# A hybrid attention and mixture-of-experts block on one core: the shared expert's first two token chunks are placed between the two halves of the routing logits

## The chip, the cores and the metric

The kernel runs on one core of one Trainium2 chip. The metric is the device time of one execution in microseconds (us), the median of three runs. One further execution was taken by the hardware profiler; all durations below come from that one.

## The reference, cut to what matters

Eleven layers run one after the other on 2 x 1024 tokens of width 128: three attentions of a first block with two Fourier feed-forwards, then a location attention, a mixture of experts, a masked linear layer, a ReLU attention, a feed-forward with ReLU, and a second mixture of experts. The change touches the two mixture-of-experts layers only. Each computes, in float32, with `xt` the layer-normed tokens:

```python
scores = jax.nn.sigmoid(xt @ gate_w.T)                 # 16 experts
_, idx = lax.top_k(scores + gate_b, 4)
w = take_along_axis(scores, idx); w = w / sum(w) * 2.5
comb = zeros((T, 16)).at[arange(T)[:, None], idx].add(w)
def expert_body(y, (w13_e, w2_e, c_e)):
    h = silu_and_mul(xt @ w13_e.T)                     # 128 -> 2 x 64
    return y + c_e[:, None] * (h @ w2_e.T)
y = scan over the 16 experts
y = y + silu_and_mul(xt @ w13_s.T) @ w2_s.T            # the shared expert, no routing
```

## The kernel before, in words

Activations lie transposed, width on the 128 partitions and tokens along the free axis, in four chunks of 512 tokens. It is written by hand, one instruction stream for each engine, with named semaphores; each engine runs its stream in program order. The streams are below `@block.tensor` (TensorE, `pe`), `@block.scalar` (ScalarE, `act`), `@block.vector` (VectorE, `dve`), `@block.gpsimd` (GpSimd, `pool`) and `@block.sync` (SyncE, `sp`, which issues the DMAs). Every matmul but a transpose goes through the helper `mm` at line 1639, so the profile knows them all by that line and they are told apart by operands and shape. A float32 matmul of the program is two MATMULs in the profile.

A mixture-of-experts layer (`moe_layer`, called "layer 1" for i = 0 and "layer 2" for i = 1) follows a layer norm. The norm leaves its centred chunk c in PSUM bank c and its variance in bank 4 + c; VectorE multiplies bank c by the factor into `z` (line 1158) and counts `n_z`, so `n_z` at 4n + c + 1 says that chunk c of `z` is there and that bank c may be overwritten.

TensorE then runs, in this order:
- the routing logits, lines 2030 to 2036: for each of 16 tiles of 128 tokens a matmul with `z` as the stationary side and `gate_w` (16 columns) moving, all into bank 4; `n_z` is waited for at the first tile of each chunk, and the last matmul counts `m_log`;
- `ahead(a)` for a = 0 to 9 (lines 2041 to 2052). For a = 0 and 1 this is the shared expert's gate and up projections of token chunks 2a and 2a + 1, 64 output rows each, into the halves of bank a (gate) and bank 2 + a (up); for a = 2 to 9 it is the gate and up projection of expert pair a - 2 for chunk 0. From a = 2 on it waits for `e_a`, which ScalarE counts when it has emptied the banks of a - 2. Each ends with a count on `e_gu`;
- after `ahead(5)`, `ahead(6)` and `ahead(7)` the `route_rows` (line 2069): transposes (line 2072) of the combine weights of chunks 0 and 1, of chunk 2, and of chunk 3. They wait for `m_d`, which VectorE counts through the 12 steps of the routing;
- the loop over `PAIRS`: gate and up projections of chunks 1 to 3 (`gate_up`), the shared expert's down projection (`shared_down`, once per chunk, which waits for `m_cs`) and the experts' down projections (`down`).

ScalarE (line 1043) waits for `m_log`, takes the exponential of the 16 x 16 logits (line 1045), then for each a applies SiLU to the gate bank (line 1057) and copies the up bank (line 1058, counts `e_a`). A table load stands before the first SiLU. Behind a = 6, 7, 8 it copies the transposed combine weights (line 1050, counts `m_cs`). GpSimd (line 753) multiplies the two results into the hidden rows, one product for each a. VectorE (lines 1499 to 1530) turns the exponentials into combine weights: add, reciprocal, bias, top-8 for each of 16 tiles (1509), match-and-replace for each (1517), compare (1520), products, sum, reciprocal, and a last scaling (1528). It then starts the loop over `PAIRS` with line 1553, hidden rows times the combine weights that SyncE has stored to DRAM and loaded back spread over 64 partitions (lines 550 to 575).

Of the kernel before, what the change touches and what calls it, by code (L numbers as in the profile page):

```python
# [31 lines left out]
T = B * S  # L32
# [3 lines left out]
P = 128  # L36
# [15 lines left out]
NE, INTER, TOPK = 16, 64, 4  # L52
# [50 lines left out]
def build(nc, xt, wp, vp, cp, bp, rope_q, rope_k, bias_q, bias_k, out):  # L103
    ctx = ExitStack()
    with ctx:
# [3 lines left out]
        def sem(name):  # L109
            return ctx.enter_context(nc.semaphore(name))  # L110
# [4 lines left out]
        h, z = hz[:, 0:T], hz[:, T:2 * T]  # L115
# [61 lines left out]
        def bank(i):  # L177
            return ps[:, i, :]
# [4 lines left out]
        def w_(name, rows=P):  # L183
            a, b = WAT[name]
            return wsb[0:rows, a:b]
# [11 lines left out]
        def c_(name, rows=P):  # L197
            a, b = CAT[name]
            return csb[0:rows, a:b]
# [8 lines left out]
        def ch(t, c):  # L208
            return t[:, c * CH:(c + 1) * CH]
# [14 lines left out]
        s_late = sem("late_weights_and_constants_loaded")  # L224
# [11 lines left out]
        n_z = sem("norm_done")  # L236
# [33 lines left out]
        m_log = sem("route_logits")  # L270
# [21 lines left out]
            mm=sem("proj_in_psum"),  # L292
            t=sem("rope_products"),
# [129 lines left out]
        def full(i, c, j):  # L423

            return (i * (NC - 1) + c - 1) * NPAIR + j
# [21 lines left out]
        AHEAD = 2 + NPAIR  # L447
# [44 lines left out]
        def weights_of(v):  # L492

            return work[:, (4 + v % 3) * S:(5 + v % 3) * S]
# [1142 lines left out]
        def _(pe):  # L1637
            def mm(o, l, r, start=True, stop=True):
                return nc.tensor.matmul(o, l, r, start=start, stop=stop, skip_group_check=True)  # L1639
# [387 lines left out]
                    mm(bank(4 + c), lhs, ch(z, c)).then_inc(s_lin, 1)  # L2027

            def moe_layer(i, n):
                for t in range(T // P):  # L2030
                    if i + t == 0:
                        pe.wait_ge(s_late, 32)
                    if t % 4 == 0:
                        pe.wait_ge(n_z, 4 * n + t // 4 + 1)
                    ins = mm(bank(4)[:, t * NE:(t + 1) * NE], z[:, t * P:(t + 1) * P], w_("gate_w"))
                ins.then_inc(m_log, 1)

                wg, wu = [w_(name)[:, NPAIR * P:NPAIR * P + INTER] for name in ("w_gate", "w_up")]
                wd = w_("w_down")[:, NPAIR * P:NPAIR * P + P]

                def ahead(a):

                    if a >= 2:
                        pe.wait_ge(e_a, AHEAD * i + a - 1)
                    if a < 2:
                        for o, w in ((bank(a), wg), (bank(2 + a), wu)):
                            for half in range(2):
                                ins = mm(o[HB * half:HB * (half + 1)], w, ch(z, 2 * a + half))
                    else:
                        mm(bank(a % 2), w_("w_gate")[:, (a - 2) * P:(a - 1) * P], ch(z, 0))  # L2050
                        ins = mm(bank(2 + a % 2), w_("w_up")[:, (a - 2) * P:(a - 1) * P], ch(z, 0))
                    ins.then_inc(e_gu, 1)

                def shared_down(c):

                    rows = slice(INTER * (c % 2), INTER * (c % 2 + 1))
                    pe.wait_ge(e_m, AHEAD * i + c // 2 + 1)
                    mm(bank(4 + c), wd[rows], moe[rows, 5, c // 2], True, False)

                def gate_up(c, j):  # L2060
                    f = full(i, c, j)
                    if c == 1 and j < 2:
                        pe.wait_ge(e_a, AHEAD * (i + 1))
                    else:
                        pe.wait_ge(m_su, f - 1)
                    mm(bank(f % 2), w_("w_gate")[:, j * P:(j + 1) * P], ch(z, c))
                    mm(bank(2 + f % 2), w_("w_up")[:, j * P:(j + 1) * P], ch(z, c)).then_inc(m_gu, 1)

                def route_rows(c):
                    pe.wait_ge(m_d, ROUTE_STEPS * (i + 1))  # L2070
                    for tt in range(4):
                        ins = nc.tensor.transpose(bank(4 + c)[0:NE, tt * P:(tt + 1) * P],  # L2072
                                                  rt[:, (4 * c + tt) * NE:(4 * c + tt + 1) * NE], c_("ident"))
                    ins.then_inc(m_t, 1)

                def down(n):
                    c, j = PAIRS[n]
                    k = ITEMS * i + n
                    pe.wait_ge(m_h, k + 1)
                    return mm(bank(4 + c), w_("w_down")[:, j * P:(j + 1) * P], moe[:, 2, k % 2], False, j == NPAIR - 1)  # L2080

                if i == 0:
                    pe.wait_ge(s_ws, 16)
                for a in range(AHEAD):
                    ahead(a)
                    for c in ROUTE_AT.get(a, ()):
                        route_rows(c)
                for n, (c, j) in enumerate(PAIRS):
                    if c or n == 0:
                        for ahead_of in [p for p in PAIRS[n + 1:] if p[0]][0:1]:  # L2090
                            gate_up(*ahead_of)
                    if j == 0:
                        pe.wait_ge(m_cs, NC * i + c + 1)
                        shared_down(c)
                    down(n).then_inc(m_y if j < NPAIR - 1 else s_lin, 1)
# [25 lines left out]
            for c in range(NC):  # L2121
                pe.wait_ge(n_z, 4 * 6 + c + 1)
                mm(bank(c), w_("loc_w"), ch(z, c)).then_inc(l_xt, 1)
                for tt in range(4):
                    t = 4 * c + tt
                    ins = nc.tensor.transpose(bank(4 + c)[:, tt * P:(tt + 1) * P], z[:, t * P:(t + 1) * P],
                                              c_("ident"))
# [3 lines left out]
            for v in range(B * KT + 2):  # L2131
                if v < B * KT:
# [3 lines left out]
                    for half in range(2):  # L2136
                        ins = mm(bank(2 * (v % 2) + half), z[:, v * P:(v + 1) * P], ch(xtr, CB * b + half))
                    ins.then_inc(l_s, 1)
                if v >= 2:
# [3 lines left out]
                    for half in range(2):  # L2143
                        ins = mm(bank(4 + CB * b + half), zr[:, u, :],
                                 weights_of(u)[:, half * CH:(half + 1) * CH], u % KT == 0, u % KT == KT - 1)
# [3 lines left out]
            for c in range(NC):  # L2149
                ins = mm(bank(0)[32 * c:32 * c + 32], c_("ones")[:, 0:32], ch(dacc, c))  # L2150
            ins.then_inc(l_den, 1)
            pe.wait_ge(d_v, 1)
            for c in range(NC):
                mm(bank(c), c_("first_row")[32 * c:32 * c + 32], inverse[32 * c:32 * c + 32]).then_inc(d_r, 1)
            norm(7)
            moe_layer(0, 7)
            norm(8)
            pe.wait_ge(s_fb, 7)
# [6 lines left out]
            for c in range(NC):  # L2165
# [7 lines left out]
                for j in range(FF // P):  # L2173
                    pe.wait_ge(f_r, 4 * c + j + 1)
                    ins = mm(bank(4 + c), w_("ff2")[:, j * P:(j + 1) * P], ffh[:, c % 2, j], j == 0, j == 3)
                ins.then_inc(s_lin, 1)
            norm(12)
            moe_layer(1, 12)


# [190 lines left out]
```

## Time and profile before

| | |
|---|---|
| median of 3 runs | 1020.58 us (1020.56 to 1021.92) |
| profiled execution, its own time | 1023.21 us |
| its span in the trace | 1021.1 us |
| mean granted TensorE clock | 0.948 of full |
| TensorE busy | 948.7 us, 93% |
| VectorE / ScalarE / GpSimd busy | 535.3 (52%) / 540.0 (53%) / 147.7 (14%) us |
| the first mixture-of-experts layer's logits start | at 570.3 us of the span |
| the second one's | at 916.5 us |

The span is the time between the first and the last instruction in the trace; the execution's own time has 2.1 us around it. PEclk is the share of the full TensorE clock of 2.4 GHz that was granted in a stretch, so 0.50 is 1.2 GHz. "Busy" counts an engine as busy while an instruction is on it, however little of it the instruction uses. A timeline row merges neighbouring instructions of one kind; where other engines' instructions come between, a merged row can span them, and its duration includes the last one's run to its end.

### The profile page before, as it was taken

How to read it: one execution, taken by the hardware profiler on the slowest of the kernel's cores; microseconds unless marked ns; L12 is line 12 of the kernel's file. 1: busy time of each engine (PE TensorE's matmuls, PEld its weight loads, DVE VectorE, ACT ScalarE, POOL GpSimd, SP SyncE). 2: the span in 40 equal slices, each digit the busy share in tenths (PEclk: the TensorE clock that was granted, in tenths of full speed). 3: DMA queues.
4: the chain of work that ended last, by engine and by line, in shares of the span. 5: the costliest groups of instructions: out<-in, count | busy, mean ns of one | idle time of the engine just before them, and what ended most of it. 6: DMA issues, size and time to landing. Idle time of an engine off the chain costs nothing.

```text
span 1021.1 us, 22819 instructions
## 1 busy us (share of the span) xinstructions
PE 948.7 (93%) x9990; PEld 436.0 (43%) x9990; DVE 535.3 (52%) x870; ACT 540.0 (53%) x767; POOL 147.7 (14%) x164
## 2 busy tenths in 40 slices
PE   7698978999999988988998999989999999999998
PEld 4476733433333335754443444434333333444443
DVE  4576545523324375665565525555666666423554
ACT  6044535889999856443765531256455454445121
POOL 3001120501001003120010120000223322004000
PEclk9899989899999997589998799999999999899999
DMA  7644050100000000000000057100000000001651
GB/s 205 215 128 125 7 218 0 42 2 2 2 2 2 2 1 1 3 3 2 0 1 0 1 135 138 62 1 1 2 2 2 2 2 2 0 1 43 160 123 52
DMA packets 16763, 43.16 MB, mean 42 GB/s; under 512 B 4844, under 2 KB 5292, under 8 KB 15244
## 3 DMA queue, kind: packets, MB, share of 16 engines
q1 hardware_dynamic: 15692, 39.51, 14.5%
q10 hardware_dynamic: 972, 2.20, 0.7%
q8 instruction: 79, 1.29, 0.5%
q14 instruction: 20, 0.16, 0.1%
HBM read 36.91 MB, written 4.55 MB: 41 GB/s over the span
## 4 chain that ended last, share of the span: by engine, by line
PE 82%; ACT 8%; DVE 6%; issue 2%; DMA 1%; POOL 1%; ACTq 0%; SPq 0%; DVEq 0%; POOLq 0%
PE ps L1639 82%; ACT nrr L816 1%; ACT nrr L818 1%; ACT nsq L809 1%; DVE mxq L1258 1%; ACT work L897 1%; POOL work L677 1%; ACT nrr L826 0%; ACT nrr L823 0%; DMA stf<-scr_k 0%; DVE aux L1451 0%; DVE work L1307 0%; DMA x<-in_x 0%; PE ps L2072 0%; DVE work L1363 0%
## 5 line engine op out<-in xcount | busy, mean ns | idle before, releaser
L1639 PE MATMUL ps<-rq,stf 32*64 32x512 f32 (+4 forms) x4096 | 208.4, 465 | 3.3 <-ACT hz L1001 1.6
L1639 PE MATMUL ps<-work,vbuf 64*32 64x128 f32 (+6 forms) x2992 | 195.5, 421 | 2.4 <-DVE nsq L1357 2.2
L1639 PE MATMUL ps<-hz,wsb 128*128 128x512 f32 (+1 forms) x352 | 161.9, 624 | 5.0 <-ACT nsq L842 2.5
L957 ACT ACTIVATE work<-ps 128x1024 f32<-128x1024 f32 x144 | 139.5, 1021 | 14.3 <-PE ps L1639 10.4
L1639 PEld LDWEIGHTS ps<-rq,stf 32*64 32x64 f32 x4096 | 97.5, 147 | 110.2 <-issue 84.1
L1019 ACT ACTIVATE work<-ps 128x1024 f32<-128x1024 f32 x72 | 73.6, 1024 | 75.7 <-PE ps L1639 75.7
L1639 PEld LDWEIGHTS ps<-work,vbuf 64*32 64x32 f32 (+1 forms) x2992 | 62.9, 111 | 116.1 <-issue 64.4
L1639 PEld LDWEIGHTS ps<-hz,wsb 128*128 128x128 f32 (+1 forms) x352 | 62.8, 192 | 85.3 <-issue 73.2
L1341 DVE TENSOR_TENSOR work<-work,csb 128x1024 f32<-128x1024 f32 (+1 forms) x40 | 40.7, 1018 | 97.2 <-ACT work L957 96.8
L1065 ACT ACTIVATE work<-ps 128x512 f32<-128x512 f32 x48 | 28.7, 597 | 117.2 <-PE ps L1639 117.2
L1639 PE MATMUL ps<-work,wsb 128*128 128x512 f32 (+1 forms) x176 | 87.0, 603 | 2.7 <-DVE work L1553 2.7
L1402 DVE TENSOR_SCALAR work<-ps 128x1024 f32<-128x1024 f32 (+3 forms) x72 | 68.5, 952 | 24.2 <-PE ps L1639 24.2
L897 ACT ACTIVATE work<-ps 128x512 f32<-128x512 f32 x64 | 37.4, 598 | 65.3 <-PE ps L1639 65.3
L1550 DVE TENSOR_TENSOR work<-ps,work 128x512 f32<-128x512 f32 x48 | 33.2, 691 | 64.0 <-ACT work L1065 40.8
L1639 PE MATMUL ps<-bsb 128*64 128x512 bf16 x256 | 53.1, 398 | 13.8 <-DMA stf<-scr_k 7.4
L1639 PE MATMUL ps<-nsq,csb 128*128 128x512 f32 (+3 forms) x152 | 53.3, 530 | 10.8 <-DVE nrr L1253 3.0
L809 ACT ACTIVATE nsq<-ps 128x512 f32<-128x512 f32 x40 | 23.5, 588 | 62.4 <-PE ps L1639 62.4
L1258 DVE TENSOR_REDUCE mxq<-ps 128x4 f32<-128x512 f32 x64 | 42.8, 688 | 22.3 <-PE ps L1639 21.3
L1639 PEld LDWEIGHTS ps<-work,wsb 128*128 128x128 f32 (+1 forms) x176 | 31.9, 189 | 50.0 <-issue 34.3
L738 POOL TENSOR_TENSOR work<-work,csb 128x512 f32<-128x512 f32 (+1 forms) x40 | 36.4, 911 | 106.7 <-ACT work L1019 106.7
L719 POOL TENSOR_SCALAR aux<-nsq,csb 128x1024 f32<-128x1024 f32 x8 | 24.2, 3025 | 156.8 <-DVE nsq L1328 110.4
L1639 PE MATMUL ps<-x,csb 128*128 128x512 f32 x64 | 35.6, 663 | 6.3 <-DMA x<-in_x 4.8
(200 smaller groups left out, 1172.9 us busy)
## 6 DMA issues: line engine op xcount, KB each, us to landing
stf<-scr_w SPq DMA_DIRECT2D x32, 256.0 KB, 4.5
stf<-scr_w SPq DMA_DIRECT2D x64, 128.0 KB, 3.3
stf<-scr_q SPq DMA_DIRECT2D x12, 192.0 KB
wsb<-in_w SPq DMA_DIRECT2D x1, 2192.0 KB, 12.5
rq<-in_rq SPq DMA_DIRECT2D x2, 1024.0 KB, 9.9
stf<-scr_k SPq DMA_DIRECT2D x9, 204.0 KB
rq<-scr_k SPq DMA_DIRECT2D x6, 204.0 KB
hz<-scr_k SPq DMA_DIRECT2D x6, 204.0 KB
```

The costliest lines, as they stand in the source:

```text
L719: nc.gpsimd.tensor_scalar(nums[:, b * S:(b + 1) * S], half_out[0][:, b * S:(b + 1) * S], c_("part")[:, 0:1], None, ALU.mult).then_inc(q["s ...
L738: nc.gpsimd.tensor_tensor(cells, cells, c_("keep").unsqueeze(1).unsqueeze(1) .broadcast_to(list(cells.shape)), ALU.mult).then_inc(q["mk"], 1)
L809: nc.scalar.activation(nsq[:, c], bank(c), ACT.Square).then_inc(n_sq, 1)
L897: nc.scalar.activation(prob[:, st, hd], bank(n % 2), ACT.Exp, scale=SCALE).then_inc(q["ex"], 1)
L957: nc.scalar.activation(probs_of(n)[:, 2 * k:2 * k + 2].rearrange("p h s -> p (h s)"), two(slot(2 * n + k)), ACT.Exp, scale=SCALE).then_inc ...
L1019: nc.scalar.activation(probs_of(n)[:, 0:2].rearrange("p h s -> p (h s)"), two(slot(2 * n)), ACT.Relu, scale=SCALE).then_inc(q["ex"], 1)
L1065: nc.scalar.activation(moe[:, 0, f % 2], bank(f % 2), ACT.Silu).then_inc(m_sg, 1)
L1258: nc.vector.tensor_reduce(mxq[:, k % 2, 4 * u:4 * u + 4], bank(4 + m % 2).rearrange("p (t s) -> p t s", t=4), AX.X, ALU.max).then_inc(w_m, 1)
L1341: nc.vector.tensor_tensor(cells, cells, c_("keep").unsqueeze(1).unsqueeze(1) .broadcast_to(list(cells.shape)), ALU.mult).then_inc(q["mk"], 1)
L1402: ins = nc.vector.tensor_scalar(to[:, :, lo:hi], src[:, :, lo:hi], SCALE, 0.0, ALU.mult, ALU.max)
L1550: nc.vector.tensor_tensor(product, bank(2 + f % 2), moe[:, 0, f % 2], ALU.mult).then_inc(m_su, 1)
L1639: return nc.tensor.matmul(o, l, r, start=start, stop=stop, skip_group_check=True)
```

## The change

The logits are no longer one run of 16 tiles. A function `logits(c)` issues the four tiles of chunk c, waiting for that chunk of `z`. The new order is: logits of chunks 0 and 1; a wait for `n_z` at 4n + 3, which is chunk 2 of `z` (bank 2, into which `ahead(0)` writes, held chunk 2's centred values); `ahead(0)`, the shared expert's gate and up for token chunks 0 and 1; logits of chunks 2 and 3, with the count on `m_log`; then `ahead(1)` to `ahead(9)` as before. In layer 1 the waits for the late weights (`s_late`) and for the copied shared down weights (`s_ws`) both stand ahead of the logits. The streams of the other engines, the DMAs and every instruction's operands are the same as before.

```diff
--- before.py
+++ after.py
@@ -2027,14 +2027,6 @@
                     mm(bank(4 + c), lhs, ch(z, c)).then_inc(s_lin, 1)
 
             def moe_layer(i, n):
-                for t in range(T // P):
-                    if i + t == 0:
-                        pe.wait_ge(s_late, 32)
-                    if t % 4 == 0:
-                        pe.wait_ge(n_z, 4 * n + t // 4 + 1)
-                    ins = mm(bank(4)[:, t * NE:(t + 1) * NE], z[:, t * P:(t + 1) * P], w_("gate_w"))
-                ins.then_inc(m_log, 1)
-
                 wg, wu = [w_(name)[:, NPAIR * P:NPAIR * P + INTER] for name in ("w_gate", "w_up")]
                 wd = w_("w_down")[:, NPAIR * P:NPAIR * P + P]
 
@@ -2079,9 +2071,22 @@
                     pe.wait_ge(m_h, k + 1)
                     return mm(bank(4 + c), w_("w_down")[:, j * P:(j + 1) * P], moe[:, 2, k % 2], False, j == NPAIR - 1)
 
+                def logits(c):
+                    pe.wait_ge(n_z, 4 * n + c + 1)
+                    for t in range(4 * c, 4 * c + 4):
+                        ins = mm(bank(4)[:, t * NE:(t + 1) * NE], z[:, t * P:(t + 1) * P], w_("gate_w"))
+                    return ins
+
                 if i == 0:
+                    pe.wait_ge(s_late, 32)
                     pe.wait_ge(s_ws, 16)
-                for a in range(AHEAD):
+                logits(0)
+                logits(1)
+                pe.wait_ge(n_z, 4 * n + 3)
+                ahead(0)
+                logits(2)
+                logits(3).then_inc(m_log, 1)
+                for a in range(1, AHEAD):
                     ahead(a)
                     for c in ROUTE_AT.get(a, ()):
                         route_rows(c)
```

## Rows read from the trace of the kernel before

**Rows 1.** The page, part 4: shares of the chain that ended last, by engine
```profile
PE 82%; ACT 8%; DVE 6%; issue 2%; DMA 1%; POOL 1%; ACTq 0%; SPq 0%; DVEq 0%; POOLq 0%
```

**Rows 2.** Chain of waits, layer 2: start us, us, engine and line, instructions
```profile
915.58 16.95 PE ps L1639 x66
```

**Rows 3.** Windows of 1 us, layer 2: busy (instructions) by engine, PEclk, DMA
```profile
919.00:920.00 1.00, 1.00 (x11) 1.00 (x10) 0.00 (x0) 0.00 (x0) 0.00 (x0) 1.00 0.00 0
920.00:921.00 1.00, 1.00 (x6) 0.42 (x7) 0.37 (x2) 0.77 (x2) 0.00 (x0) 0.92 0.00 0
...
924.00:925.00 1.00, 1.00 (x6) 0.14 (x2) 0.89 (x12) 0.23 (x1) 0.69 (x1) 0.87 0.00 0
```

**Rows 4.** Windows of 1 us, layer 1, same columns
```profile
572.00:573.00 1.00, 1.00 (x10) 1.00 (x9) 0.56 (x1) 0.00 (x0) 0.00 (x0) 0.84 0.00 0
573.00:574.00 1.00, 1.00 (x7) 1.00 (x6) 0.00 (x0) 0.00 (x0) 0.00 (x0) 0.50 0.07 16
...
579.00:580.00 1.00, 1.00 (x6) 0.38 (x4) 0.89 (x12) 0.69 (x2) 0.23 (x1) 0.74 0.00 0
```

**Rows 5.** Timeline, layer 2: start, us, engine, line, operation, count [idle before <-releaser]
```profile
916.54 3.64 PE L1639 MATMUL ps<-wsb,hz 128*128 128x16 f32 x32
...
916.79 0.69 DVE L1158 TENSOR_TENSOR hz<-ps,nrr 128x512 f32<-128x512 f32 x1 [1.03 <-ACT nrr L818]
...
918.12 0.69 DVE L1158 TENSOR_TENSOR hz<-ps,nrr 128x512 f32<-128x512 f32 x1 [0.63 <-ACT nrr L818]
...
920.22 0.38 ACT L1045 ACTIVATE stf<-ps 128x256 f32<-128x256 f32 x1 [2.13 <-PE ps L1639]
...
920.62 1.28 ACT L1057 ACT_TABLE_LOAD   x1
...
923.15 0.60 ACT L1057 ACTIVATE work<-ps 128x512 f32<-128x512 f32 x1 [1.25 <-PE ps L1639]
...
923.64 0.59 ACT L1058 ACTIVATE work<-ps 128x512 f32<-128x512 f32 x1
...
925.51 0.60 ACT L1057 ACTIVATE work<-ps 128x512 f32<-128x512 f32 x1 [1.27 <-PE ps L1639]
...
929.45 0.67 DVE L1528 SCALAR_TENSOR_TENSOR stf<-stf 128x256 f32<-128x256 f32 x1
...
930.84 0.60 ACT L1057 ACTIVATE work<-ps 128x512 f32<-128x512 f32 x1 [0.63 <-PE ps L1639]
...
932.56 0.60 ACT L1057 ACTIVATE work<-ps 128x512 f32<-128x512 f32 x1 [0.63 <-PE ps L1639]
...
943.93 0.69 DVE L1553 TENSOR_TENSOR work<-aux,stf 128x512 f32<-128x512 f32 x1 [13.81 <-DMA stf<-scr_w]
```

**Rows 6.** Timeline, layer 1
```profile
570.29 4.66 PE L1639 MATMUL ps<-wsb,hz 128*128 128x16 f32 x32
...
574.98 0.38 ACT L1045 ACTIVATE stf<-ps 128x256 f32<-128x256 f32 x1 [3.14 <-PE ps L1639]
...
580.86 0.60 ACT L1057 ACTIVATE work<-ps 128x512 f32<-128x512 f32 x1 [1.17 <-PE ps L1639]
...
582.09 1.48 DVE L1520 TENSOR_TENSOR stf<-stf 128x256 f32<-128x256 f32 x1
...
584.80 0.67 DVE L1528 SCALAR_TENSOR_TENSOR stf<-stf 128x256 f32<-128x256 f32 x1
...
587.91 0.60 ACT L1057 ACTIVATE work<-ps 128x512 f32<-128x512 f32 x1 [0.63 <-PE ps L1639]
```

**Rows 7.** Timeline, TensorE after gaps: 2.49 us at 684.88, 1.18 us at 942.32
```profile
684.88 3.32 PE L1639 MATMUL ps<-hz,wsb 128*128 128x512 f32 x4 [2.49 <-ACT nsq L842]
...
942.32 1.98 PE L1639 MATMUL ps<-hz,wsb 128*128 128x512 f32 x4 [1.18 <-ACT work L1058]
```

**Rows 8.** Windows over and behind those two gaps
```profile
685.00:686.00 1.00, 1.00 (x2) 0.43 (x3) 0.60 (x2) 1.00 (x3) 0.00 (x0) 0.66 0.00 0
...
940.00:945.00 5.00, 3.83 (x9) 1.16 (x7) 0.69 (x1) 2.69 (x6) 2.53 (x2) 1.00 0.96 228
```

## The prediction, made before the changed kernel was built or run

> **What bounds the kernel now.** I read the page first: TensorE holds 82% of the chain that ended last [rows 1]. The chain around the second expert layer then shows one unbroken TensorE piece of 16.95 us from the end of the norm through the logits into the experts [rows 2]. ScalarE, VectorE and GpSimd work beside it. So in the changed stretch the time is TensorE's program order, and only a delay that reaches TensorE counts. The windows show what TensorE loses there. From 919 to 920 it is busy 1.00, all of it logits, at clock 1.00; from 920 to 921 the mean clock is 0.92, so the fall to 1.2 GHz comes at 920.84; from 924 to 925 it is 0.87, so 2.4 GHz is back at 924.26. That is 3.42 us at half speed [rows 3]. In layer 1 the same reading gives 572.68 to 579.52, 6.84 us [rows 4]. In layer 1 the fall comes 2.39 us into the logits, in layer 2 it comes 0.73 us behind the end of 3.57 us of them [rows 5, 6]: each time right after a run of 16-column matmuls.
>
> Layer 2: the logits start at 916.54, and the exponential, always 0.11 behind its matmul, starts at 920.22; so the logits take until 920.11, 3.57 us at full clock. `ahead(0)` and `ahead(1)` end 0.11 before the SiLU at 925.51: 925.40, which is 5.29 us [rows 5]. At full clock they would need 3.44: an `ahead` of four 128-row MATMULs takes 1.72 (SiLU to SiLU, 930.84 to 932.56 [rows 5]), and the eight 64-row ones run two at a time, for 5.29 us less half of 3.42 is 3.58, near eight steps of 0.43 and far from sixteen. `ahead(5)` ends at 932.45. With a full clock it would be 916.54 + 3.57 + 3.44 + 4 x 1.72 = 930.43: layer 2 loses 2.02 us. Layer 1: start 570.29, `ahead(5)` ends at 587.80 [rows 6], against 570.29 + 13.89 = 584.18: 3.62 us lost. Together 5.6 us are there to be won.
>
> **The change part by part.** Nothing is added: the same matmuls in another order, and no DMA or other queue is passed.
>
> *Logits of chunks 0 and 1* start as before, half of 3.57 is 1.79: in layer 2 until 918.33. *The new wait for chunk 2 of `z`*: VectorE writes it until 916.79 + 0.69 = 917.48 [rows 5], so TensorE, with everything queued behind it, does not stop. The moved waits for late weights cost nothing; those loads were issued long before 570 us and `ahead(0)` followed the logits without a gap. *`ahead(0)`*: 1.72 at full clock, until 920.05. *Logits of chunks 2 and 3*: chunk 3 is ready at 918.81 [rows 5], no wait; until 921.84. The count on `m_log` therefore comes 5.30 after the start instead of 3.57, **1.73 us later**. That is the price, and everyone behind `m_log` pays it: ScalarE (exponential, table load, SiLU of `ahead(0)`, since its order is fixed) and VectorE's routing.
>
> *ScalarE.* The table load ends at 920.62 + 1.28 = 921.90, 1.79 after `m_log`; SiLU and copy take 924.23 - 923.15 = 1.08 [rows 5]. `ahead(2)` needs that copy: at `m_log` + 2.93, with 0.06 to start. `ahead(1)` is over after 1.72, so TensorE idles 1.2 us where it had none. `ahead(5)` then ends at `m_log` + 2.93 + 6.88 = + 9.81.
>
> *VectorE.* The combine weights are ready at 929.45 + 0.67 = 930.12, 10.01 after `m_log` [rows 5]. In layer 1 it is 584.80 + 0.67 = 585.47, 10.60 after 574.87 [rows 6]; the compare alone takes 1.48 there [rows 6], beside a product of GpSimd. The transposes used to find them ready for 2.33 us in either layer (932.45 less 930.12, 587.80 less 585.47). That cover hid the routing, and it is gone: the transposes now start at `m_log` + 10.1 or + 10.7, later than TensorE's own 9.81.
>
> *Sum.* Layer 2: 921.84 + 10.1 = 931.95 against 932.45, **0.5 us won**. Layer 1: 570.29 + 5.30 + 10.7 = 586.29 against 587.80, **1.5 us won**. Behind the transposes everything keeps its distance: the products of `ahead(9)`, for which `gate_up` waits at 942.32 [rows 7], and the store and loads that VectorE awaits until 943.93 [rows 5] all hang on them. Bounds: VectorE's chain of 10.6 in both layers gives 1.4 in all, of 10.0 in both 2.6; a chain under 9.81 lets ScalarE's bound rule, 3.2. I take each layer's own chain: 2.0, from the profiled 1021.1 us of span to 1019.1, and 1023.21 to 1021.2. The median of the timed runs lies 2.63 below the profiled execution. Part of that may be lighter falls of the clock than the trace has (half of a 3.42 us stretch is 1.71), and then less can be won. I take 0.6 off for it: 1020.58 - 1.4 = **1019.2**.
>
> **A rule against the change.** The rows show TensorE busy 1.00 up to the fall [rows 3], so the kind of work brought the clock down, not a gap. The Trainium skill (TensorE: Matmul & The Clock Gate, "Why this matters for your kernels") has it that the clock is kept by leaving no idle gaps in TensorE's work; by that the logits would never have cost a thing, the split would buy nothing, and only the price would stay, 1023.6 as in rival A. The trace disagrees with it in both layers.
>
> **The rivals.**
> *A, the routing becomes the bound and there is little clock to win (slower).* Where the clock would have held anyway, `ahead(5)` ends at start + 13.89 before, and the transposes start at + 15.4 after: 1.5 us worse in that layer, from the wait of `route_rows`. It decides as soon as the old order loses under 1.5 us in a layer. For it: layer 2 loses only 2.02. Against: both layers of the trace are past that point. Both layers so: 1020.58 + 3.0 = 1023.6; one so, the other as in the trace: about 1020.6. By the Trainium skill (same page, "Part 1: The HAM clock gate") the monitor runs free of the kernel, so the spot of a fall varies between executions; no row here shows that.
> *B, the clock falls all the same.* The thin matmuls are as many as before. Against: the longest stretch of them shrinks from 3.57 to 1.79 us, and around an idle gap of 1.18 us [rows 7] the clock stayed at 1.00 [rows 8]. For: after a gap of 2.49 us at 684.88 [rows 7] it fell (0.66 in that microsecond [rows 8]), and the new order has a gap of 1.2 us besides. A fall in the middle doubles the second half of the logits, 1.8 more ahead of everything: 1021.0 with one layer, 1022.8 with both.
> *C, falls elsewhere move.* All after 575 us shifts by a microsecond or two; a fall such as that at 685 costs half of 3.42, so 1.7 either way: 1017.5 or 1020.9.
>
> **How the numbers follow.** The clock holds and both layers win: 0.52. A: 0.20 (0.13 one layer, 0.07 both). B: 0.15. C: 0.13. A measurement of this kernel tells 0.2% from no change, 2.04 us: below 1018.5 is faster, above 1022.6 slower. The forecast case passes that line with a chain of 10.0 or falls as long as in layer 1: 0.18 of its 0.52; C adds 0.05: faster 0.23. Slower: A in both 0.07, B 0.05, C 0.02: 0.14. The rest, 0.63, is the same. The range goes from 1017.5 (the bound of 3.2, or C) up to 1022.4, short of A in both layers.
>
> **What would show it.** The clock at 1.00 from the start of the logits to `gate_up` in both layers; the exponential 5.4 us after the logits' start; a TensorE gap of 1.2 us ended by ScalarE's copy (line 1058) ahead of `ahead(2)`; the transposes waiting for line 1528 instead of following `ahead(5)` at once; `gate_up` 1.5 and another 0.5 us earlier. A half clock between the halves of the logits, or transposes that find their weights ready for a microsecond and more, would make this wrong.

## The result and the profile after

| | before | changed |
|---|---|---|
| first comparison: median (range, executions) | 1019.83 us (1015.01 to 1021.92, 8) | 1013.25 us (1010.76 to 1015.78, 8) |
| ratio, 95% interval | | 0.9938, 0.9917 to 0.9959 |
| the same comparison a second and a third time | | 0.9960 (0.9935 to 0.9985), 0.9926 (0.9898 to 0.9954) |
| profiled execution: time, span | 1023.21, 1021.1 us | 1012.53, 1010.4 us |
| mean granted TensorE clock | 0.948 | 0.962 |

The changed kernel is faster by 0.4 to 0.7% in the three comparisons; over all executions it has a median of 1012.95 us (32 of them) against 1018.49 us (93), 5.5 us less. I had forecast 1.4 us, and a range from 1017.5 up. Executions of one kernel spread over more than 10 us (the kernel before from 1012.3 to 1026.9), far more than the first three showed. So a single time says little here, and the traces, compared stretch by stretch, say much.

Windows of 2 us over layer 1 and one over layer 2 of the changed kernel (busy by engine, then PEclk, in the columns of [rows 3]):

```profile
564.00:566.00 2.00, 2.00 (x17) 1.40 (x18) 0.91 (x2) 0.78 (x2) 0.00 (x0) 1.00 0.03 8
566.00:568.00 2.00, 2.00 (x16) 1.19 (x12) 0.00 (x0) 0.00 (x0) 0.00 (x0) 1.00 0.00 0
568.00:570.00 2.00, 2.00 (x14) 1.26 (x15) 0.64 (x3) 1.07 (x2) 0.00 (x0) 1.00 0.00 0
...
909.00:911.00 2.00, 2.00 (x16) 1.19 (x13) 0.00 (x0) 0.00 (x0) 0.00 (x0) 1.00 0.00 0
```

TensorE is as busy as it was in [rows 3, 4], with the same thin matmuls, and the clock stays at 1.00. The timeline of layer 1 of the changed kernel, and one line of its layer 2:

```profile
563.27 1.85 PE L1639 MATMUL ps<-wsb,hz 128*128 128x16 f32 x16
...
565.05 1.94 PE L1639 MATMUL ps<-hz,wsb 128*64 128x512 f32 x8
...
566.92 1.96 PE L1639 MATMUL ps<-wsb,hz 128*128 128x16 f32 x16
...
568.91 0.38 ACT L1045 ACTIVATE stf<-ps 128x256 f32<-128x256 f32 x1 [4.10 <-PE ps L1639]
...
570.61 0.60 ACT L1057 ACTIVATE work<-ps 128x512 f32<-128x512 f32 x1
...
571.75 7.13 PE L1639 MATMUL ps<-hz,wsb 128*128 128x512 f32 x16 [1.01 <-ACT work L1058]
...
576.02 0.46 DVE L1520 TENSOR_TENSOR stf<-stf 128x256 f32<-128x256 f32 x1
...
577.72 0.63 DVE L1528 SCALAR_TENSOR_TENSOR stf<-stf 128x256 f32<-128x256 f32 x1
...
578.92 0.60 ACT L1057 ACTIVATE work<-ps 128x512 f32<-128x512 f32 x1 [0.63 <-PE ps L1639]
...
588.68 1.98 PE L1639 MATMUL ps<-hz,wsb 128*128 128x512 f32 x4 [1.18 <-ACT work L1058]
...
921.37 0.09 PEld L2064 LDWEIGHTS ps<-csb,stf 128*16 128x16 f32 x1 [0.36 <-DVE stf L1528]
```

The logits start at 563.27, `ahead(0)` stands between their halves, the exponential comes 5.64 us after the start, ScalarE is at `ahead(0)` 7.34 us after the start (570.61; it was 8.31 in layer 1 before, where the clock was low, and 6.61 in layer 2), and `ahead(2)` starts at 571.75 after a gap of 1.01 us that ScalarE's copy ends. `gate_up` starts at 588.68. I call **the layer's length** the time from the first logits MATMUL to the first MATMUL of `gate_up`: 25.41 us here, and 25.41 in layer 2 (906.23 to 931.64). Before it was 27.38 (570.29 to 597.67) and 25.78 (916.54 to 942.32, [rows 5, 7]). The two layers together save 2.34 us, where the prediction's sum had 2.0. The two spans differ by 10.7 us, so most of the difference of this pair lies elsewhere: 7.0 us of it ahead of layer 1 (570.29 against 563.27), where no instruction is changed.

### The profile page after: what moved, and what is told of

It reads as the page before. It is cut to its first block, busy times and chain, and to the rows that moved or that the text cites. A ratio compares the mean times of both kernels' runs of the same rounds, so it can differ in the third digit from the quotient of the medians.

```text
span 1010.4 us, 22819 instructions
## 1 busy us (share of the span) xinstructions
PE 935.3 (93%) x9990; PEld 429.2 (42%) x9990; DVE 534.3 (53%) x870; ACT 539.9 (53%) x767; POOL 146.6 (15%) x164
## 4 chain that ended last, share of the span: by engine, by line
PE 81%; ACT 9%; DVE 6%; issue 2%; DMA 1%; POOL 1%; ACTq 0%; SPq 0%; DVEq 0%; POOLq 0%
PE ps L1639 80%; ACT nrr L816 1%; ACT nrr L818 1%; ACT nsq L809 1%; DVE mxq L1258 1%; ACT work L897 1%; DVE work L1363 1%; POOL work L677 1%; ACT nrr L826 0%; DMA stf<-scr_k 0%; ACT nrr L823 0%; ACT work L986 0%; DVE aux L1451 0%; DVE work L1307 0%; PE ps L2064 0%
## 5 line engine op out<-in xcount | busy, mean ns | idle before, releaser
L1639 PE MATMUL ps<-rq,stf 32*64 32x512 f32 (+4 forms) x4096 | 206.3, 459 | 3.9 <-ACT hz L1001 1.6
L1639 PE MATMUL ps<-work,vbuf 64*32 64x128 f32 (+6 forms) x2992 | 192.3, 414 | 1.6 <-DVE nrr L1357 1.0
L1639 PE MATMUL ps<-hz,wsb 128*128 128x512 f32 (+1 forms) x352 | 157.9, 597 | 7.0 <-ACT work L1058 4.4
L957 ACT ACTIVATE work<-ps 128x1024 f32<-128x1024 f32 x144 | 139.3, 1022 | 13.5 <-PE ps L1639 10.2
L1065 ACT ACTIVATE work<-ps 128x512 f32<-128x512 f32 x48 | 28.7, 597 | 117.2 <-PE ps L1639 117.2
L1397 DVE SCALAR_TENSOR_TENSOR work<-ps,csb 128x256 f32<-128x256 f32 x64 | 24.9, 420 | 30.4 <-PE ps L1639 30.4
```

What stands on the lines that cost most here:

```text
L957: nc.scalar.activation(probs_of(n)[:, 2 * k:2 * k + 2].rearrange("p h s -> p (h s)"), two(slot(2 * n + k)), ACT.Exp, scale=SCALE).then_inc ...
L1065: nc.scalar.activation(moe[:, 0, f % 2], bank(f % 2), ACT.Silu).then_inc(m_sg, 1)
L1397: nc.vector.scalar_tensor_tensor(out=to[:, :, off:off + P], in0=src[:, :, off:off + P], scalar=0.0, in1=c_("keep_s").unsqueeze(1).broadcas ...
```

## The experiments

### The same two kernels again, and each layer by itself

Where do the missing microseconds come from? Four kernels ran beside the kernel before. Their edits: none (`before_again`, the kernel before; `after_again`, the changed one), and the split in one layer alone:

```diff
-                pe.wait_ge(n_z, 4 * n + 3)
-                ahead(0)
+                if i == 0:                      # layer1_only; i == 1 in layer2_only
+                    pe.wait_ge(n_z, 4 * n + 3)
+                    ahead(0)
                 logits(2)
                 logits(3).then_inc(m_log, 1)
-                for a in range(1, AHEAD):
+                for a in range(int(i == 0), AHEAD):
```

Expected of the kernel before, run as a candidate:

> The kernel before, unchanged, run as a candidate. Two theories of the 6 us. Theory L (the layers, and chance): the change itself is worth 2 to 3 us in the two layers, and the rest is clock falls elsewhere that come and go between executions. Then this kernel measures 1.000 of the kernel before, within 0.2%, its first logits start anywhere between 563 and 571 us of the span, and its layers (start of the logits to the first gate_up) take 25.8 to 27.4 us each, differently in the two. Theory S (something systematic outside the layers): its first logits start at 570 us again, and never near 563.

Expected of the changed kernel:

> The changed kernel once more. Theory L: both layers take 25.4 us (start of the logits to the first gate_up) with the clock at 1.00 from the one to the other, whatever the clock does elsewhere; the first logits start anywhere between 563 and 571 us; the ratio is 0.996 to 0.998. Theory S: the first logits start at 563 us again and the ratio is 0.994.

Expected of the split in layer 1 alone:

> The split of the logits in layer 1 alone. Theory L: layer 1 takes 25.4 us, layer 2 25.8 to 27.4 us, the time lies half way, 0.997 to 0.999 of before. Theory S: the stretch ahead of layer 1 is as short as with both (563 us), ratio 0.994 to 0.996.

Expected of the split in layer 2 alone:

> The split in layer 2 alone. Theory L: layer 2 takes 25.4 us, layer 1 25.8 to 27.4 us, the time 0.997 to 0.999 of before. Theory S, with its cause in layer 1's code: nothing ahead of layer 1 moves, the first logits start at 570 us, ratio above 0.998.

Measured: `before_again` 1017.58 us, ratio 1.0005 (0.9976 to 1.0034); `after_again` 1014.25, 0.9960 (0.9935 to 0.9985); `layer1_only` 1015.50, 0.9962 (0.9931 to 0.9992); `layer2_only` 1016.87, 0.9984 (0.9962 to 1.0007). Each median is of 12 executions. The table has the stretches of all traces of this study in us, those of the kernels further down too. "1019 to 1113" runs from the first start of line 1019, the ReLU attention's first copy, to the first of line 1113, the feed-forward; it holds no changed instruction.

| kernel | span | first logits at | layer 1 | layer 2 | 1019 to 1113 |
|---|---|---|---|---|---|
| before | 1021.1 | 570.29 | 27.38 | 25.78 | 173.5 |
| before_again | 1010.9 | 560.12 | 27.38 | 25.78 | 173.4 |
| changed | 1010.4 | 563.27 | 25.41 | 25.41 | 171.9 |
| after_again | 1008.0 | 562.99 | 25.41 | 25.41 | 170.5 |
| after_third | 1006.9 | 561.87 | 25.41 | 25.41 | 170.5 |
| layer1_only | 1018.3 | 571.26 | 25.41 | 27.41 | 170.5 |
| layer2_only | 1017.8 | 567.44 | 27.38 | 25.41 | 173.5 |
| before_padded | 1019.6 | 569.26 | 27.39 | 27.40 | 170.5 |
| after_padded | 1015.8 | 565.37 | 25.41 | 25.41 | 173.5 |
| gate_between | 1017.8 | 571.12 | 24.55 | 27.63 | 170.5 |
| gate1_ahead2 | 1010.0 | 565.51 | 24.56 | 25.41 | 170.5 |
| spare_between | 1011.2 | 564.87 | 26.05 | 26.05 | 170.5 |
| three_one | 1014.8 | 564.51 | 27.04 | 25.41 | 173.6 |
| ahead_first | 1021.8 | 574.89 | 25.74 (see below) | 24.12 | 170.5 |

Two things are seen. First, the time of the first logits swings from 560 to 571 us in unsplit and split kernels alike, and theory S falls: `before_again` starts them at 560.12, earlier than any split kernel (and outside the 563 to 571 that theory L gave). That is the spread between executions. It stems from ahead of layer 1: the first start to the last of line 986, in the global attention, takes 53.0 us in the trace of before, 46.4 in `before_again`, 46.5 in `after_again` and 53.0 in `layer1_only`. The windows over it, in before and in `before_again`:

```profile
398.00:451.00 53.00, 49.27 (x1293) 36.13 (x1296) 34.03 (x26) 26.68 (x39) 8.24 (x3) 0.60 0.01 3
```

```profile
395.00:441.40 46.40, 38.16 (x1276) 28.80 (x1284) 34.45 (x26) 26.28 (x38) 8.13 (x3) 0.83 0.01 4
```

The granted clock is 0.60 in the long one and 0.83 in the short one (and 0.83 in `after_again`, 0.60 in `layer1_only`): the swing too is time at the low clock. Second, **the layers themselves do not swing** between executions of one kernel. The timeline of layer 1 in `before_again`, TensorE alone:

```profile
560.12 4.76 PE L1639 MATMUL ps<-wsb,hz 128*128 128x16 f32 x32
...
587.50 1.98 PE L1639 MATMUL ps<-hz,wsb 128*128 128x512 f32 x4 [1.17 <-ACT work L1058]
```

From 560.12 to 587.50 is 27.38 us, as in the trace of before, though its span is 10.2 us shorter.

Theory L is right about the layers and half wrong about the rest. The last column is not chance: it is 173.4 or 173.5 in the three traces whose layer 1 is that of the kernel before, with nothing moved behind it, and 170.5 to 171.9 in the four that have the changed kernel's layer 1 and no padding (changed, `after_again`, `after_third`, `layer1_only`). For the pair of `before_again` and `after_again` the sum is: layer 1 1.97, layer 2 0.37, last column 2.9, and 0.4 from layer 1's `gate_up` to line 1019 (111.5 against 111.1): 5.6 us, close to the 5.5 by which the pooled medians differ. (That the prediction had "5.6 us to be won" inside the two layers is a coincidence: these give 2.34.) The spans differ by 2.9 only, since the split kernel happened to come to layer 1 2.87 us later. Layer 1's split alone gives 1.97 + 3.3 and gives back 1.6 in layer 2, which is 27.41 in it: 3.7 us, 0.9964 against the measured 0.9962. Layer 2's alone gives 0.37, 0.9996, within 0.9962 to 1.0007.

### Do the falls hang together? Work added for nothing

Windows of 25 us of the kernel before, over the norm and the gap behind layer 1 and over the end of the ReLU attention, and the two lines that bound the last column:

```profile
673.00:698.00 25.00, 22.08 (x47) 8.54 (x46) 15.12 (x24) 19.25 (x33) 0.00 (x0) 0.93 0.00 1
857.60:882.60 25.00, 22.76 (x144) 9.34 (x140) 14.43 (x25) 10.85 (x20) 1.73 (x2) 0.86 0.00 1
```

```profile
L1019 ACT ACTIVATE work<-ps x72: 1019/1023/1027, 709.1 to 858.8; 128x1024 f32<-128x1024 f32 x72
...
L1113 ACT ACTIVATE work<-ps,vsb x16: 669/687/687, 882.6 to 905.9; 128x512 f32<-128x512 f32 x16
```

The same of `after_again`:

```profile
663.50:688.50 25.00, 21.03 (x48) 8.28 (x47) 15.28 (x24) 19.26 (x33) 0.00 (x0) 1.00 0.00 1
845.00:870.00 25.00, 22.70 (x180) 8.83 (x172) 16.06 (x27) 12.82 (x22) 1.73 (x2) 1.00 0.00 1
```

```profile
L1019 ACT ACTIVATE work<-ps x72: 1017/1024/1028, 699.5 to 849.1; 128x1024 f32<-128x1024 f32 x72
...
L1113 ACT ACTIVATE work<-ps,vsb x16: 670/687/688, 870.0 to 893.2; 128x512 f32<-128x512 f32 x16
```

Before, PEclk is 0.93 and 0.86 there; in `after_again` it is 1.00 in both, in unchanged code. (The second window of each ends at the first start of line 1113; at the lower clock TensorE gets through 144 matmuls in it, against 180.) The gap of 2.5 us ahead of 684.88 in [rows 7], right behind which the clock falls, is there in `after_again` too (2.50 us ahead of 675.61), and the clock holds through it. So a gap of 2.5 us does not decide by itself; where it stands against the clock's earlier changes may. If so, moving the work must do what the split does. One edit, in TensorE's norm, repeats the first centring matmul behind layer 1, whose result is written over by the real one:

```diff
                         wait_source(pe, n, c)
+                        if n == 8 and c == 0:
+                            for width in (512, 320):        # (512, 512, 176) in after_padded
+                                mm(bank(0)[:, 0:width], c_("center"), src[:, 0:width])
                         mm(bank(c), c_("center"), ch(src, c)).then_inc(n_cen, 1)
```

Expected of the kernel before with 1.4 us of it:

> The kernel before, with 1.4 us of TensorE work added for nothing between layer 1 and the next norm (its first centring matmul is done three times, 512, 320 and 512 columns wide). Theory G (the falls hang together): what the split saves outside the layers comes from where the work behind layer 1 stands relative to the clock's last rise; in the unsplit traces layer 1 starts its gate_up 18.3 us after a rise, and the clock then falls at the 2.5 us gap behind the layer and again at the end of the ReLU attention; in two of the split ones neither fall comes. Moving the work 1.4 us later should do the same without any split: layer 1 still 27.38 us, no low stretch at the gap, none or a short one at the end of the ReLU attention (start of line 1019 to start of line 1113: 170.5 instead of 173.5), net 1.4 added and 3.4 saved, so 2 us faster, ratio 0.998. Rival R (those falls are random): the padding costs 1.4 us, ratio 1.0014, and the two falls are there.

Expected of the changed kernel with 2.0 us of it:

> The changed kernel with 2.0 us of TensorE work added for nothing at the same place. Theory G: both layers stay at 25.41, but the two falls behind layer 1 come back, 173.5 us from line 1019 to line 1113; 2.0 added and 3.4 lost, ratio to the kernel before 0.999 to 1.001. Rival R: 2.0 us slower than the changed kernel, ratio 0.996 to 0.998, and falls as before in some traces.

Measured: `before_padded` 1018.58 us, 0.9972 (0.9947 to 0.9998), `after_padded` 1018.79 us, 0.9995 (0.9970 to 1.0020). Windows and bounds of `before_padded`:

```profile
672.00:697.00 25.00, 21.05 (x48) 8.42 (x47) 14.22 (x23) 18.34 (x32) 0.00 (x0) 1.00 0.00 1
854.60:879.60 25.00, 22.69 (x180) 8.81 (x172) 16.07 (x27) 12.82 (x22) 1.73 (x2) 1.00 0.01 2
```

```profile
L1019 ACT ACTIVATE work<-ps x72: 1018/1023/1027, 709.1 to 858.7; 128x1024 f32<-128x1024 f32 x72
...
L1113 ACT ACTIVATE work<-ps,vsb x16: 670/687/687, 879.6 to 902.8; 128x512 f32<-128x512 f32 x16
```

and of `after_padded`:

```profile
666.00:691.00 25.00, 22.08 (x48) 8.78 (x47) 13.29 (x21) 17.21 (x30) 0.00 (x0) 0.93 0.00 1
852.70:877.70 25.00, 22.76 (x144) 9.33 (x140) 14.47 (x25) 10.90 (x20) 1.73 (x2) 0.86 0.00 1
```

```profile
L1019 ACT ACTIVATE work<-ps x72: 1018/1023/1027, 704.2 to 853.9; 128x1024 f32<-128x1024 f32 x72
...
L1113 ACT ACTIVATE work<-ps,vsb x16: 670/687/687, 877.7 to 900.9; 128x512 f32<-128x512 f32 x16
```

Both go as theory G has it: 1.4 us of useless work take both falls out of the unsplit kernel (1.00, 1.00, 879.6 - 709.1 = 170.5), 2.0 us bring both back into the split one (0.93, 0.86, 877.7 - 704.2 = 173.5), with layer 1 at 27.39 and 25.41 as before. What I missed is layer 2 of `before_padded`: its fall grows, 27.40 instead of 25.78, as in `layer1_only`. By the trace the padding wins 3.0, and loses 0.95 and 1.62: 0.4 us, not 2. The interval just holds that (0.9996) and excludes the rival's 1.0014. `after_padded` loses 2.3 and 3.0, 5.3 us of the 5.6 that the change had won.

The padding does not shorten the gap: it is 2.49 us long in both padded kernels. What differs is how far its end lies behind the last rise of the clock. Over the 14 traces, with the rises read from PEclk as in the prediction, the clock fell at the gap where this was 105.4 to 105.5 us (three traces), 108.5, 116.2 (two), 118.5 and 119.1, and held where it was 103.3, 106.8, 117.1 to 117.2 (three) and 117.7. The kernel before stands at 105.4, and 1.4 us of padding take it to 106.8; `after_again` stands at 117.1, and the padded changed kernel at 119.1. A microsecond or two decide, in either direction.

So the saving outside the layers is real and belongs to the change, but through the clock alone: with the fall in layer 1 gone, what comes later stands elsewhere against the clock.

### Is it the unbroken run of thin matmuls?

`ahead_first` has `ahead(0)` ahead of all the logits:

```diff
-                logits(0)
-                logits(1)
                 pe.wait_ge(n_z, 4 * n + 3)
                 ahead(0)
+                logits(0)
+                logits(1)
                 logits(2)
```

> ahead(0) ahead of all four chunks of logits, in both layers: the same order for ScalarE and the same late count as in the changed kernel, but the logits in one run of 3.57 us. If the unbroken run is what brings the clock down, the clock falls in both layers and they take 27 us or more. If the split gained by having work of the experts done early, they take 25.4 to 26.4 us at a clock of 1.00 (0.9 more than the changed kernel, since ahead(0) has to wait for chunk 2 of z).

It took 1023.94 us (one execution). Windows of 1 us around the logits, and TensorE's timeline in layer 1:

```profile
577.00:578.00 1.00, 1.00 (x10) 1.00 (x9) 0.00 (x0) 0.00 (x0) 0.00 (x0) 0.86 0.00 0
...
922.00:923.00 1.00, 1.00 (x9) 0.95 (x10) 0.00 (x0) 0.20 (x1) 0.00 (x0) 0.73 0.00 0
```

```profile
573.02 1.94 PE L1639 MATMUL ps<-hz,wsb 128*64 128x512 f32 x8 [0.93 <-DVE hz L1158]
574.89 4.47 PE L1639 MATMUL ps<-wsb,hz 128*128 128x16 f32 x32
...
600.63 1.55 PE L1639 MATMUL ps<-hz,wsb 128*128 128x512 f32 x3 [1.18 <-ACT work L1058]
```

The clock falls in both layers inside the logits. From where the norm's last matmul is done, which is where the logits would start otherwise (571.9, by the same distance from its start as in the changed kernel), `gate_up` at 600.63 is 28.7 us away, and 27.0 in layer 2 (916.1 to 943.05): the 27 and more expected of the run theory, and out of reach of the other. (The table's 25.74 and 24.12 run from the first logits, and so leave out `ahead(0)`, which stands ahead of them here.)

`spare_between` keeps the split but throws away what stands in the gap, and does `ahead(0)` where it used to be:

```diff
                 pe.wait_ge(n_z, 4 * n + 3)
-                ahead(0)
+                for o, w in ((bank(0), wg), (bank(2), wu)):
+                    for half in range(2):
+                        mm(o[HB * half:HB * (half + 1)], w, ch(z, half))
                 logits(2)
                 logits(3).then_inc(m_log, 1)
-                for a in range(1, AHEAD):
+                for a in range(AHEAD):
```

> The split with spare work: between the two halves of the logits stands a copy of ahead(0) whose results are thrown away, and ahead(0) itself follows where it was. If the clock is what the change buys, the layers take 25.9 us (0.5 more than the changed kernel: ahead(0) and ahead(1) after the count take 3.4, ScalarE's bound is 2.9) at clock 1.00, though 1.72 us of TensorE work were added to the kernel before in each. If early work of the experts is what it buys, they take 27.5 us or more (25.8 and 1.7).

1013.33 us (one execution); windows over the whole of both layers, and TensorE's timeline in layer 1:

```profile
564.00:592.00 28.00, 26.82 (x109) 13.35 (x110) 10.74 (x61) 16.71 (x30) 12.58 (x10) 1.00 0.12 29
906.00:933.00 27.00, 25.82 (x108) 12.82 (x107) 10.64 (x60) 16.23 (x29) 12.09 (x10) 1.00 0.11 25
```

```profile
564.87 1.85 PE L1639 MATMUL ps<-wsb,hz 128*128 128x16 f32 x16
566.65 1.94 PE L1639 MATMUL ps<-hz,wsb 128*64 128x512 f32 x8
568.52 1.96 PE L1639 MATMUL ps<-wsb,hz 128*128 128x16 f32 x16
570.41 5.14 PE L1639 MATMUL ps<-hz,wsb 128*64 128x512 f32 x19
```

Clock 1.00 through both layers, and 26.05 us each. The extra `ahead(0)` costs 0.64 over the changed kernel (0.5 expected). Layer 1 of the kernel before took 27.38 with less work. So the change buys the clock. That it does work of the experts early is worth the 0.64 us: little in layer 1, but in layer 2, where the kernel before took 25.78, the split with spare work would lose 0.27.

### How thin may it be? Less dense work, or a longer run

`gate_between` puts only the gate half of `ahead(0)` (0.86 us) between the halves of the logits and the up half behind them; `gate1_ahead2` does so in layer 1 and keeps the changed kernel's order in layer 2; `three_one` has all of `ahead(0)` between chunks 2 and 3:

```diff
                 logits(0)
                 logits(1)
-                pe.wait_ge(n_z, 4 * n + 3)
-                ahead(0)
+                half(bank(0), wg)
                 logits(2)
                 logits(3).then_inc(m_log, 1)
+                half(bank(2), wu).then_inc(e_gu, 1)
                 for a in range(1, AHEAD):
```

where `half(o, w)` is the two 64-row matmuls of one weight. Expected of `gate_between`:

> The changed kernel with only the gate half of the shared expert's first product between the two halves of the logits (0.86 us of dense work instead of 1.72), the up half behind them. The count of the logits comes 0.86 us earlier. Theory 1 (a dense piece between is what matters): clock 1.00, layers 24.5 us, 1.8 us faster than the changed kernel, ratio 0.994. Theory 2 (the share of dense work matters; 0.86 between twice 1.79 us of thin matmuls is too little): the clock falls in or right behind the logits of one layer or both, that layer takes 26 us or more, and the time is that of the changed kernel or worse.

Expected of `gate1_ahead2`, which ran beside the changed kernel on one chip:

> Layer 1 with only the gate half between (24.55 in the trace of gate_between, where the clock held), layer 2 with all of ahead(0) (25.41). If the clock holds in layer 1 again, this is 0.86 us ahead of the changed kernel there, and 0 to 1 us in all, since the work behind layer 1 moves against the clock; ratio 0.993 to 0.996. If it falls in layer 1, that layer takes 26 us or more and the falls behind it are those of an unsplit layer: ratio 0.996 to 0.999.

Expected of the changed kernel beside it:

> The changed kernel a third time, for a third trace and beside the next kernel on one chip. Both layers 25.41 us at clock 1.00 again; from line 1019 to line 1113 170.5 to 172; ratio 0.994 to 0.996.

Expected of `three_one`:

> ahead(0) between chunks 2 and 3 of the logits: runs of 2.68 and 0.89 us of thin matmuls instead of twice 1.79. The same count and the same 25.4 us if the clock holds; if a run of 2.7 us is already too long, the clock falls in a layer and it takes 26 us or more. I expect a fall in one layer of the two.

Measured: `gate_between` 1015.24 us, 0.9956 (0.9928 to 0.9984); `gate1_ahead2` 1011.40 us, 0.9936 (0.9905 to 0.9967); `after_third` 1012.16 us, 0.9926 (0.9898 to 0.9954); `three_one` 1016.96 us (one execution). Windows of `gate_between`, layer 1 from the end of its logits and the fall in layer 2:

```profile
575.00:597.00 22.00, 20.68 (x71) 9.41 (x71) 8.63 (x58) 14.31 (x26) 12.79 (x10) 1.00 0.17 39
...
914.00:915.00 1.00, 1.00 (x8) 0.77 (x7) 0.00 (x0) 0.00 (x0) 0.00 (x0) 0.92 0.00 0
915.00:917.00 2.00, 2.00 (x11) 2.00 (x11) 0.00 (x0) 0.00 (x0) 0.00 (x0) 0.50 0.00 0
```

Windows of `three_one`, the fall in layer 1 and layer 2 as a whole:

```profile
566.00:567.00 1.00, 1.00 (x11) 1.00 (x10) 0.69 (x1) 0.06 (x1) 0.00 (x0) 0.93 0.06 16
567.00:569.00 2.00, 2.00 (x7) 0.92 (x8) 0.00 (x0) 0.00 (x0) 0.00 (x0) 0.50 0.00 0
910.00:936.00 26.00, 23.88 (x98) 11.97 (x96) 10.02 (x60) 16.38 (x30) 11.52 (x9) 1.00 0.08 20
```

With 0.86 us of dense work between, layer 1 takes 24.55 us at 1.00, the 0.86 us that the earlier count promised, but in layer 2 the clock falls in the third chunk's logits and the layer takes 27.63. A run of 2.68 us falls in layer 1 (27.04) and holds in layer 2 (25.41). Over all traces:

| thin matmuls at a stretch | dense work between | layers where the clock held |
|---|---|---|
| 3.57 us, unbroken | none | 0 of 10 |
| 2.68 and 0.89 us | `ahead(0)` | 1 of 2 |
| twice 1.79 us | half of `ahead(0)` | 2 of 3 |
| twice 1.79 us | all of `ahead(0)`, or its copy | 13 of 13 |

The layers of one row are not independent draws. In layer 1 the logits start 4.4 to 4.6 us behind a rise of the clock in 12 of the 14 traces (565.86 to 570.29 in before; 5.9 in the changed kernel's first trace, 7.4 in `ahead_first`), so layer 1 is mostly one case repeated. In layer 2 the distance is 43 to 45, 225 or 334 to 346 us. The best evidence is in pairs at one distance. In layer 2 of before, 43.5 us behind the rise at 873.06, the clock fell; in layer 2 of `layer2_only`, 43.5 us behind the rise at 870.18, it held. Here are the windows of the two rises and that of `layer2_only`'s layer 2; the fall in before is in [rows 3]:

```profile
873.00:874.00 1.00, 1.00 (x3) 0.42 (x3) 0.76 (x2) 0.00 (x0) 0.00 (x0) 0.97 0.00 0
```

```profile
870.00:871.00 1.00, 1.00 (x4) 0.49 (x3) 0.75 (x1) 0.00 (x0) 0.00 (x0) 0.91 0.00 0
...
913.66:939.07 25.41, 23.23 (x98) 11.80 (x96) 10.02 (x60) 15.77 (x29) 11.54 (x9) 1.00 0.09 24
```

Likewise 345.3 us behind a rise: the clock fell in layer 2 of `layer1_only`, unsplit, and held in that of `after_again`, split.

`gate1_ahead2` should have been the best: layer 1 is 24.56 again. Its median is 0.8 us lower than that of `after_third`, its ratio 0.001 higher; the intervals overlap almost wholly, so whether it beats the changed kernel isn't settled. Its trace has a low stretch from 677.1 at the gap behind layer 1, where `after_third` has none: `gate_up` of layer 1 to line 1019 takes 111.3 us instead of 111.0, which gives back 0.3 of the 0.86 us. `after_third` itself came out better than expected (0.9926 against 0.994 to 0.996).

## Why the prediction was wrong

- *Where the time is lost.* Right: the logits bring the clock down at a TensorE busy of 1.00, and split they do not. The rule of the Trainium skill that was weighed there (TensorE: Matmul & The Clock Gate, "Why this matters for your kernels") would, as the prediction applied it, have left only the price of the late count. The traces do not bear that out: 0 of 10 unbroken runs kept the clock though TensorE had no gap.
- *The price.* The count came 5.53 us after the start, not 5.30: `ahead(0)` holds the second half back by 1.87 (565.05 to 566.92), not 1.72, and that half takes 1.88, not 1.79. `ahead(2)` started 2.95 behind the count (571.75 less 568.80), 2.93 forecast.
- *VectorE's chain* was mis-sized: 9.55 us (577.72 + 0.63 less 568.80), not 10.01 or 10.60. The compare on line 1520 took 0.46, where it took 1.48 in [rows 6]; GpSimd's product lies over it for 0.18 us instead of 1.20. So the cover of 2.33 us did go, but it ended nearly in a tie, and not with VectorE as the bound: the weight load of the transposes sat idle 0.34 us (0.36 in layer 2) until line 1528 was done, while TensorE was still on `ahead(5)`. `ahead(5)` ended 10.0 us behind the count (9.81 forecast), and it is this path, through ScalarE's copy, that set the layer. Layer 1 won 1.97 (1.5 forecast), layer 2 0.37 (0.5).
- *The 0.6 us taken off* was the first wrong step. I read the 2.63 us between the profiled execution and the median as lighter falls in the layers. The layers are 27.38 and 25.78 at spans of 1021.1 and 1010.9 alike; the spread sits ahead of them.
- *Rival C* was the step that failed most. The sum of 1.4 us put the falls elsewhere at nothing; as a rival I had named them, at 1.7 us of either sign, drawn anew each time, with a chance of 0.13. They are more than half of the result, 3.3 us: the fall at the gap at 685 and a longer one at the end of the ReLU attention, which stands in the trace of before and in no term of my sum. Their sign was the same in the traces as long as nothing else moved the work. The sentence of the Trainium skill (same page, "Part 1: The HAM clock gate") that the monitor runs free of the kernel made me treat all falls as drawn anew in each execution. The traces show less freedom: layer 1 is 27.38 or 27.39 in all four unsplit ones. My reading, which the two padded kernels and the distances at the gap support but do not prove, is that each rise of the clock puts the work in step with it again, and that it runs alike from there to the next change.
- *The starting value.* 1020.58, the median of three, was itself 2.1 us above the pooled 1018.49. Of the 5.95 us between the forecast 1019.2 and the measured 1013.25 these 2.1 are chance; 3.3 are the falls elsewhere, and what is left, 0.5, is the 0.6 taken off and 0.3 more won in the layers, less a few tenths of spread. From 1018.49 the range would have gone down to 1015.4, and still not to the result.
- *Rival A* did not decide: its price was paid (ScalarE's gap of 1.0 us, the late count), but both layers were past its point. *Rival B* did not come about in any of the 13 layers with a whole `ahead(0)` or its copy in the middle; with less there, or a longer run, it did (two layers of five).
- *The line of 0.2%* for what a measurement can tell came from three executions within 1.4 us of each other. With 12 and 35 executions the intervals are still 0.25% to each side.

Open: why the clock stays low longer in the stretch of line 986 in one execution than in another, and in how many executions the split kernel keeps the falls behind layer 1 (it had two short ones in one trace of three). Nor was it tried whether it is the 16 columns or the weight load ahead of every matmul that brings the clock down, or whether a pause between the halves would do as well as dense work.

## What to carry to other kernels

A TensorE that is busy all the time can still lose its clock to a run of narrow matmuls; look at the granted clock behind every such run, and put dense work that has to be done anyway into the middle of it, even if what waits for the run comes later. Then price each fall of the clock in the whole span, not only the one that the edit is about, since a fall that is removed moves all that follows against the clock. Compare two traces stretch by stretch before comparing their totals: here one stretch of unchanged code differed by 7 us from one execution to the next and another by 3 us because of the change.

## What the runs showed of the hardware that was not expected

- Useless work can cost nothing or less: 1.4 us added ahead of the gap behind layer 1 left the kernel at 0.9972 (0.9947 to 0.9998; 0.4 us won by the traces), and 2.0 us added to the changed kernel cost 5.3 us by the traces.
- At a gap of 2.5 us in TensorE's work the clock fell in the traces of before and `before_again` and stayed at 1.00 in `after_again` and `layer1_only`, with the same work on both sides of it. It fell with the gap's end 105.4 us behind the clock's last rise, and held at 106.8.
- The same float32 compare of 128x256 on VectorE takes 0.42 us with no GpSimd product over it (layer 2 of `before_padded`), and 0.46, 0.89 and 1.48 us where a product lies over 0.18, 0.61 and 1.20 us of it. It is longest where the product starts just before it.
